# Attention units reordered: slot projection, output projection and gates at other places in the program

## What is computed

```python
q, k, v = heads(x @ Wq), heads(x @ Wk), heads(x @ Wv)        # 16 heads, 64 / 64 / 128 wide
s = clip(heads(x @ Ws), -32, 32)                              # 64 slots
z = cumlogsumexp(s); g = exp(z[t-1] - z[t]); p = exp(s - z)
hk = hk * g_t + k_t p_t;   ok = q_t . hk                      # key state, read by the query
pv = softmax(ok)
hv = hv * g_t + p_t v_t;   ov = pv_t . hv                     # value state
o = ov * rsqrt(mean(ov^2) + eps) * g_norm_weight
o = o * (g * sigmoid(g))                                      # g = x @ Wg
out = x + o @ Wo
```

## Time and profile before

| | |
|---|---|
| median of 3 runs | 2107.34 us (2104.89 to 2109.28) |
| the profiled execution: its time | 2111.22 us |
| the profiled execution: its span | 2109.5 us |
| PE busy | 1982.6 us, 94% of the span |
| DVE / ACT / POOL busy | 65% / 32% / 13% |
| one piece of attention weights: upper half on ACT / lower half on POOL | up to 1.07 / 2.40 us |
| granted PE clock, 1594 to 1597 / 1597 to 1600 / 1600 to 1603 us (last pair) | 0.88 / 0.50 / 0.50 |
| granted PE clock, 1639 to 1642 / 1642 to 1645 us (last pair) | 0.77 / 0.66 |
| attention, as PE sees it | from about 468 to 1681 us of the span |

### The profile page before, as it was taken

One profiled execution on the slowest core, in us unless ns is written; L12 is line 12 of the kernel. 1 busy time (PEld: TensorE's weight loads), 2 busy tenths in 40 slices (PEclk: granted clock), 3 DMA queues, 4 the chain that ended last, 5 costly groups with the idle time before them and its releaser, 6 DMA issues. The chain is left out here.

```text
span 2109.5 us, 29738 instructions
## 1 busy us (share of the span) xinstructions
PE 1982.6 (94%) x11848; PEld 1629.8 (77%) x11848; DVE 1365.2 (65%) x2702; ACT 669.6 (32%) x1207; POOL 278.8 (13%) x216
## 2 busy tenths in 40 slices
PE   2999999969999999999999999999999689999998
PEld 1788888847888888888888888888887468888786
DVE  5765667736667666666766666666767766665684
ACT  2443445514222131221222221221212144443562
POOL 3110111011011020120110110210201200110100
PEclk9999999979999999999999999999999889999999
DMA  6463436660010010010000100100100155443565
GB/s 219 131 199 120 136 119 180 204 195 9 1 38 9 1 38 8 9 31 9 21 25 1 38 9 1 38 8 1 38 1 21 40 169 191 130 110 110 150 187 183
DMA packets 54329, 165.04 MB, mean 78 GB/s; under 512 B 5424, under 2 KB 5424, under 8 KB 54192
## 3 DMA queue, kind: packets, MB, share of 16 engines
q1 hardware_dynamic: 46736, 145.80, 21.1%
q0 software_dynamic: 7456, 17.34, 4.0%
HBM read 137.40 MB, written 25.72 MB: 77 GB/s over the span
## 5 line engine op out<-in xcount | busy, mean ns | idle before, releaser
L1227 PE MATMUL at_pj<-at_w_lo,at_xT_hi 128*128 128x512 f32 x512 | 210.5, 411 | 0.0
L1227 PE MATMUL at_pj<-at_w_hi,at_xT_lo 128*128 128x512 f32 x512 | 202.3, 395 | 0.0
L1227 PE MATMUL at_pj<-at_w_hi,at_xT_hi 128*128 128x512 f32 x512 | 202.3, 395 | 0.0
L1201 PE MATMUL at_pj<-at_xT_hi,at_w_lo 128*128 128x512 f32 x384 | 158.4, 412 | 7.6 <-DVE at_gate L1004 4.9
L550 DVE TENSOR_TENSOR last_ff_w_lo<-last_ff_stage,last_ff_w_hi 128x1024 fp32r<-128x1024 f32 x80 | 97.9, 1224 | 90.4 <-ACT last_ff_w_hi L373 90.2
L1201 PE MATMUL at_pj<-at_xT_hi,at_w_hi 128*128 128x512 f32 x384 | 152.3, 397 | 0.0
L1201 PE MATMUL at_pj<-at_xT_lo,at_w_hi 128*128 128x512 f32 x384 | 151.4, 394 | 0.0
L933 ACT ACTIVATE at_ok<-at_ok 128x512 f32<-128x512 f32 x32 | 20.3, 633 | 412.2 <-DVE at_ok L1122 412.2
L550 DVE TENSOR_TENSOR first_ff_w_lo<-first_ff_stage,first_ff_w_hi 128x1024 fp32r<-128x1024 f32 x80 | 97.9, 1224 | 77.7 <-ACT first_ff_w_hi L373 76.3
L840 POOL TENSOR_TENSOR at_coef<-at_ms,minus_half 128x4 f32<-128x4 f32 x64 | 63.5, 1008 | 559.8 <-DVE at_ms L1164 559.8
L825 POOL TENSOR_TENSOR at_w_lo<-at_stage,at_w_hi 128x1024 fp32r<-128x1024 f32 (+1 forms) x36 | 78.1, 2170 | 380.3 <-ACT at_w_hi L879 380.3
(11 more groups left out here) (315 smaller groups left out, 4783.7 us busy)
## 6 DMA issues: line engine op xcount, KB each, us to landing
first_ff_stage<-wff SPq DMA_DIRECT2D x90, 512.0 KB
last_ff_stage<-wff SPq DMA_DIRECT2D x90, 512.0 KB, 3.9
at_stage<-watt SPq DMA_DIRECT2D x24, 512.0 KB, 3.7
at_stage<-watt SPq DMA_DIRECT2D x16, 384.0 KB, 3.2
xres<-x SPq DMA_DIRECT2D x4, 1024.0 KB, 9.8
mid_rows<-xres SPq DMA_DIRECT2D x4, 1024.0 KB
out<-xres SPq DMA_DIRECT2D x4, 1024.0 KB
first_ff_xg<-sorted_rows SPq DMA_DIRECT2D x3, 1028.0 KB, 5.4
```

Source lines behind the costliest of these rows:

```text
L1201: last = pe.matmul(PJ[(7 * k + part) % 2][:, :], wq(w, kk, part), x[:, kk, tok], start=(kk == 0 and n == 0), stop=(kk == KC - 1 and n == 2))
L1227: last = pe.matmul(PJ[(7 * k + 3 + t) % 2][:, :], x[:, kk, tok], wvg(w, kk), start=(kk == 0 and n == 0), stop=(kk == KC - 1 and n == 2))
```

## The change

Four moves, and their waits:

1. On PE `project_s` of the next unit stands ahead of the read of the key state (L1336), not behind it; DVE takes `s_clip` right behind the sums of the value state, and ACT takes `e_exp` right behind `q_scale`, ahead of the softmax exponential.
2. On PE `project_out` of the unit before stands behind the read of the key state, not between `project_q` and `project_k`; it writes R[0] and R[3] in place of R[2] and R[3]. DVE takes the four adds behind the scaling of the read and ahead of the maximum. The wait for `added` moves from L1326 to the softmax transposes L1350 (which write R[3]).
3. `gate_make` 2 and 3 stand ahead of both lower halves `uT_lo` on DVE, and `vg_read(3)` ahead of both upper halves on ACT.
4. On DVE `z_scan` stands behind the small product of the denominators, ahead of the masks.

```diff
 # ScalarE
                     if more:
                         q_scale(i, k + 1)
+                        e_exp(i, k + 1)
...
+                    if more:
+                        vg_read(i, k + 1, 3)
                     for b in range(2):
-                        if more and b == 1:
-                            vg_read(i, k + 1, 3)
                         act.wait_ge(u_tr, count(i, k, 2, b))
 # VectorE
-                    dve.tensor_tensor(xres[:, k * UC + cc, :], R[2 + cc % 2][:, :], xres[:, k * UC + cc, :], ALU.add).then_inc(added, 1)
+                    dve.tensor_tensor(xres[:, k * UC + cc, :], R[3 * (cc % 2)][:, :], xres[:, k * UC + cc, :], ALU.add).then_inc(added, 1)
...
                     dve.reciprocal(rzT[:, :], zT[:, :]).then_inc(rz_done, 1)
-                    if (i, k) != (0, 0):
-                        add_out(*((i, k - 1) if k else (i - 1, UNITS - 1)), last_pair and k > 0)
                     if more:
                         k_copy(i, k + 1)
...
+                    if more:
+                        s_clip(i, k + 1)
+                    dve.wait_ge(ok_mm, count(i, k, 1, 0))
+                    dve.wait_ge(rz_done, count(i, k, 1, 1))
+                    dve.tensor_tensor(pT[:, :], R[2][:, :], rzT[:, :], ALU.mult).then_inc(ok_scaled, 1)
+                    if (i, k) != (0, 0):
+                        add_out(*((i, k - 1) if k else (i - 1, UNITS - 1)), last_pair and k > 0)
...
+                    if more:
+                        z_scan(i, k + 1)
                     if last_pair and k > 0:
                         unit_statistics(k - 1)
...
+                    if more:
+                        gate_make(i, k + 1, 2)
+                        gate_make(i, k + 1, 3)
                     for b in range(2):
-                        if more and b == 1:
-                            gate_make(i, k + 1, 2)
                         dve.wait_ge(u_hi, count(i, k, 2, b + 1))
 # TensorE
                         project_q(i, k + 1)
-                    if (i, k) != (0, 0):
-                        project_out(*((i, k - 1) if k else (i - 1, UNITS - 1)), True)
-                    if more:
                         project_k(i, k + 1)
...
-                    pe.wait_ge(added, count(i, k, UC, 0))
                     pe.wait_ge(a_masked, count(i, k, 2, 2))
...
+                    if more:
+                        project_s(i, k + 1)
                     pe.wait_ge(hk_done, i * HK_AT[UNITS] + HK_AT[k + 1] + 1)
...
-                    if more:
-                        project_s(i, k + 1)
+                    if (i, k) != (0, 0):
+                        project_out(*((i, k - 1) if k else (i - 1, UNITS - 1)))
                     pe.wait_ge(ok_scaled, count(i, k, 1, 1))
...
+                    pe.wait_ge(added, count(i, k, UC, 0))
                     pe.wait_ge(pv_done, count(i, k, 1, 1))
```

More of the change, by code:

```diff
@@ L934, in pair @@
                     if more:
-                        e_exp(i, k + 1)
                         vg_read(i, k + 1, 0)
-                    if more:
                         vg_read(i, k + 1, 1)
@@ L1122, in pair @@
                     dve.tensor_tensor(by_head(ok[:, :, :]), by_head(turned_ok), spread(highest), ALU.subtract).then_inc(ok_shifted, 1)
-                    if more:
-                        s_clip(i, k + 1)
                     dve.wait_ge(pv_done, count(i, k, 1, 1))
@@ L1143, in pair @@
                         gate_make(i, k + 1, 1)
-                        z_scan(i, k + 1)
                     if last_pair and k > 0:
@@ L1181, in pair @@
                     if more:
-                        gate_make(i, k + 1, 3)
                         kn_copy(i, k + 1)
@@ L1278, in scores, with project_out @@
                             last.then_inc(a_mm, 1)
-            def project_out(i, k, next_masked):
+            def project_out(i, k):
                 if k == 0:
                     pe.wait_ge(piece_lo, i * NP + 1 + 5)
-                if next_masked:
-                    pe.wait_ge(a_masked, count(i, k + 1, 2, 2))
                 if i == PAIRS - 1 and k > 0:
@@ L1293, in project_out @@
                         for n, (x, w) in enumerate(((uT_lo, w_hi), (uT_hi, w_lo), (uT_hi, w_hi))):
-                            last = pe.matmul(R[2 + cc % 2][:, :], x[:, cc // 2, h, (cc % 2) * P:(cc % 2 + 1) * P], wo(w, h),
+                            last = pe.matmul(R[3 * (cc % 2)][:, :], x[:, cc // 2, h, (cc % 2) * P:(cc % 2 + 1) * P], wo(w, h),
                                              start=(h == 0 and n == 0), stop=(h == 1 and n == 2))
@@ L1393, in pair @@
                     else:
-                        project_out(i, k, False)
+                        project_out(i, k)
             for i in range(PAIRS):
```

3 lines of the change are left out of this document (removed).

## The result

The changed kernel takes 2078.65 us, median of four runs (2078.07 to 2081.09), beside 2108.31 us for the kernel before on the same chip (four runs, 2104.89 to 2111.34). The ratio is 0.9862, with an interval of 0.9844 to 0.9880: 29.7 us faster. 2079 had been predicted. The span of the profiled execution went from 2109.5 to 2079.3 us.

A forecast was written before the change was run, and what follows sets the result against it. PE bounds the kernel, so only its waits can go: 12.3 + 6.6 + 7.5 - 0.9 + 2.8 = 28.3 us off 2111.2 gives 2082.9, and 2079 as median. Forecast 2072 to 2084 (0.68), ends 2070 and 2093.

The forecast's parts named there:

- What bounds the kernel: PE, busy 144.53 of 146.40 us in four middle units, sets the pace; only its waits, 1.13 us a unit, can go.
- The query projection: PE's wait for gate 2 ahead of this projection, 13.0 us, goes; 12.3 us won.
- `u`: PE's wait for the second half of `u`, 0.24 us each time, goes with the scan moved: 6.6 us won.
- The key sums and the joins: PE's 0.43 us wait for the key sums goes, less 0.19 for two joins, over 31 units: 7.5 us won.
- The second join: PE leaving a float32 matmul group: the second 512 column matmul comes 0.32 behind, not 0.23; costs 0.09 us.
- The first join: PE going into a plain float32 matmul group: 0.33 us from start to start, not 0.23; costs 0.10.
- The maximum: DVE, behind the four output adds: can start at T + 1.03, T being the last output matmul's start; exponential follows.
- The cover: Slack between the softmax exponential's end and PE's weight load for the softmax transposes: 0.08 us, costed at nothing.
- rival (a): DVE's adds and maximum reach PE late: 2082 to 2098; chance 0.14 below its turning point, 0.04 beyond.
- The other queues: ACT and POOL: weight pieces delayed by `e_exp` stay hidden, piece 3 with 1.8 us to spare; no cost.
- The ends: First unit loses 0.9 us; last pair wins 2.6 and 2.4, loses 1.2 and 1: together 1.9 won.
- the clock's 0 to 4.8 us: Last pair: shorter waits may keep PE at 2.4 GHz, worth 0 to 4.8 us; 2.4 taken.

The follow-up runs named there:

- gates_only: Kernel before with only gates 2 and 3 and the fourth tanh moved ahead of the halves: 2092.66 us, ratio 0.9931.
- scan_only: Kernel before with only the scan moved ahead of the masks: 2104.68 us, ratio 0.9984.
- late_200: Changed kernel with an unused 128-column DVE addition ahead of the maximum in each unit: 2079.22 us, ratio 0.9863.
- slot_only: Kernel before with only the slot projection ahead of the key-state read, its clip and exponential moved along: 2162.80 us, ratio 1.0255.
- out_only: Kernel before with only the output projection, its adds and banks moved as in the changed kernel: 2114.72 us, ratio 1.0027.
- no_scan: Changed kernel with the scan put back behind the masks and gate 1: 2089.10 us, ratio 0.9905.
- slot_piece_first: slot_only with `e_exp` put back behind the weight pieces on ACT: 2130.72 us, ratio 1.0118 to the kernel before.
- after_again: The changed kernel run once more, nothing altered: 2078.61 us, ratio 0.9863.
- late_statistics: Changed kernel with the last tile's statistics, in the last pair, moved from ahead of the maximum to behind the subtraction: 2077.44 us, ratio 0.9849.
- best: late_statistics plus, in the very last unit, the output projection ahead of the key sums in banks 2 and 3: 2078.45 us, ratio 0.9859.
- no_slot: Changed kernel with the slot projection back behind the key-state read and output projection, `s_clip` behind the scaling: 2086.64 us, ratio 0.9895.
- late_600: Changed kernel with an unused 512-column DVE addition ahead of the maximum in each unit: 2093.54 us, ratio 0.9928.

## Why the prediction came out

**What bounds the kernel.** Right: the change took no work away and won 29.7 us. In the middle units all of it was PE's waiting; some 2 us more in the last pair are time that PE no longer spends at half clock. That the number was met to 0.4 us is in part luck: the win was 1.4 us larger than forecast, and the median of the kernel before, beside which it was measured, was 1.0 us higher than the one that the forecast started from.

**The query projection.** Forecast 12.3 us, 0.44 a unit; the steps show 0.48, and so do those of gates_only (its whole unit is 0.51 shorter). The list of waits put 0.46 there. It counts the idle time of the weight load and leaves out that a first matmul after a wait is itself drawn out: in the kernel before its second follows by 0.35 (827.49 to 827.84), in the changed kernel by 0.32.

**`u`.** 0.22 a unit against 0.24. The size was right; that it hangs on the gates' move was not seen, and scan_only showed it.

**The key sums and the joins.** 0.28 against 0.24, so right in size, and that by luck, since two errors nearly cancel. The forecast had a wait of 0.43 less 0.19 for the joins. In the steps, the value sums and the read together became shorter by 0.37, and the projections longer by 0.08. The second join was sized right: with the slot projection behind the value sums and the output projection behind the read there are two places instead of one where the second matmul comes 0.34 (792.60 to 792.94) and 0.31 (796.07 to 796.38) behind the first and not 0.23, and this costs 0.08 for the 0.09 forecast. The first join, 0.10 into the read, isn't there: PE took 0.23 into it and not the 0.33 that the earlier trace rows have into the key-state sums. And the wait was worth 0.37, not the 0.43 that the weight loads idled. The Trainium skill (TensorE: Matmul & The Clock Gate, "Step-by-step: what each phase is for") has PE pull weight loads ahead of matmuls in flight where the row groups don't conflict or where the load goes to the background weight buffer, and that would have made the joins free. The prediction told only the first of these two conditions; no run here shows which of them applies. For the step into the read the trace agrees, with 0.23; for the second matmul behind a group of another tile it doesn't, with 0.34 and 0.31.

**The maximum.** Forecast to start at T + 1.03, with T the last output matmul, and the exponential over by T + 3.11. T is 801.49, and the timelines of DVE and ACT have

```profile
801.93 0.69 DVE L1066 TENSOR_TENSOR xres<-at_r,xres 128x512 f32<-128x512 f32 x1 [0.72 <-PE at_r L1291]
802.54 0.68 DVE L1120 TENSOR_REDUCE at_highest<-at_r 128x8 f32<-128x512 f32 x1
```

```profile
803.98 0.63 ACT L934 ACTIVATE at_ok<-at_ok 128x512 f32<-128x512 f32 x1 [0.99 <-DVE at_ok L1122]
```

which is T + 1.05 and T + 3.12. The cover, 0.08 in the forecast, is 0.2: the term taken wrongly is the "some 0.2 us" that the weight load needs ahead of its matmul. It came 0.06 ahead of it in late_200 and 0.03 in late_600. This was the main reason for the chance of rival (a), which deserved less.

**The other queues.** ACT's piece 3 was reckoned hidden with 1.8 us to spare by the output projection, and no wait for `at_w_lo` shows; at the pair change near 620 us POOL is done at 622.06 and PE wants it at 623.84, 1.8 us later. slot_only shows what that cover is worth: without it, 29 us.

**The ends.** The first unit's step from the read to the transposes is 1.07 us, forecast 1.1. In the last pair (waits of PEld, 1560 to 1660 us) `at_u` fell from the 10.6 of the earlier trace rows:

```profile
PEld at_r L1385 <- DVE at_u L1167: 8.4, 6, 4.2
...
PEld at_r L1331 <- DVE at_hk L1095: 2.6, 1, 2.6
```

In steps, the transposes of `u` wait 1.36 and 1.37 us in units 1 and 2, where it was 2.69 and 2.56: 2.5 won, 2.6 forecast. The statistics cost 0.5 in each and not 0.6. Of the clock's 0 to 4.8 us I took half. Both stretches at half clock went, and these units now run at full clock (third number from the end):

```profile
1564.00:1609.00 45.00, 41.69 (x280) 34.44 (x279) 36.08 (x103) 11.95 (x26) 9.20 (x11) 1.00 0.06 24
```

But only the first stretch was worth anything. Behind the first wait for `u`, the steps of the transposes of `u`, e and the keys and of the query projection take 2.3 us more in the kernel before than in scan_only, which has the same order there and full clock. The second stretch stood at the head of the last unit, and there DVE sets the pace. There too scan_only has the order of the kernel before and full clock. These are the first transposes of `u` and the third tile of the output projection, which waits for an add on DVE, in the kernel before and then in scan_only:

```profile
1638.73 0.66 PE L1389 MATMUL at_r<-ident,at_u 128*128 128x128 f32 x4 [2.30 <-DVE at_u L1168]
...
1646.96 0.48 PE L1294 MATMUL at_r<-at_w_hi,at_uT_lo 128*128 128x512 f32 x1 [1.30 <-DVE xres L1067]
```

```profile
1632.80 0.66 PE L1390 MATMUL at_r<-ident,at_u 128*128 128x128 f32 x4 [1.12 <-DVE at_u L1169]
...
1641.03 0.47 PE L1295 MATMUL at_r<-at_w_hi,at_uT_lo 128*128 128x512 f32 x1 [2.63 <-DVE xres L1067]
```

It is 8.23 us in both: what the clock gave back there, PE waited longer for DVE. So the 2.4 us taken for the clock came out by luck: 2.3 from the first stretch and nothing from the second.

The last unit lost 1.5 and not 1, from the start of the turned keys' transposes to the last output matmul (40.3 us before, 41.8 after). PE waits ahead of the sums, ahead of the read (for the reciprocal, 3.34 us on DVE, as foreseen), and for the exponential:

```profile
1611.61 0.57 PE L1313 MATMUL at_r<-at_en,at_kn 128*64 128x64 f32 x12 [1.85 <-DVE at_kn L1008]
...
1616.08 1.18 PE L1331 MATMUL at_r<-at_qT,at_hk 128*128 128x128 f32 x8 [2.36 <-DVE at_hk L1095]
...
1627.96 1.09 PE L1346 MATMUL at_r<-ident,at_ok 128*128 128x128 f32 x4 [3.14 <-ACT at_ok L934]
```

```profile
1617.00:1620.00 3.00, 3.00 (x10) 2.37 (x9) 0.84 (x3) 0.00 (x0) 0.00 (x0) 0.51 0.00 0
```

The table of clocks was not part of the forecast for this unit, and the row above is what it missed: behind two waits close together the output projection runs at half clock for 3.4 us and takes 7.2 us instead of 5.7, so part of what it covers it pays for in its own length. The stretches at half clock that begin behind waits of this unit grew from two of 6.8 us to one of 3.4 and two of 6.8. The first unit lost 0.5 us, units 1 and 2 of the last pair won 5.1 and its last lost 1.5: 3.1 us won. With 27.7 from the middle this makes 30.8, against 30.2 between the two spans; the run-up ahead of the attention was 0.6 us longer in the trace of the changed kernel.

## What to carry to other kernels

Where one engine is busy for 98.7% of the time and its waits are short and come back in every unit, look for work that doesn't depend on what is waited for and put it ahead of the wait; then look at what that work had covered at its old place, and move something else there. Reckon such moves in pairs: the slot projection alone cost 53 us, the output projection alone 5, and together with the gates and the scan they won 30. A half clock that goes is worth nothing where another engine sets the pace behind it. Test the tight place by a delay of known size in front of it, which gives the cover in one run, and prefer the times from step to step to the idle time of the weight loads, which counts idling that costs nothing and misses matmuls that are drawn out.

## What the hardware showed beside this

- A weight load of transposes that came late, with 0.23 us of idle time ahead of it, cost PE nothing (late_200): it started 0.06 us ahead of its matmul, and the matmul was on time.
- DVE starts an instruction that depends on nothing in flight about 0.6 us behind one that takes 0.69 (801.93 to 802.54, 839.86 to 840.46), and 0.20 behind one of 128 columns that takes 0.28.
- After waits of PE of 2.55 to 2.69 us ahead of `u` in the last pair, the clock was granted at half in 11 of 12 places (the traces of before, gates_only, out_only, no_scan, slot_only and slot_piece_first have two each). After waits of 1.36 to 1.38 us it was in none of 14 (after, after_again, late_statistics, best, scan_only, no_slot and late_200), and in one of the two of late_600, where another wait of 1.34 us stands 15 us ahead of each. The one exception of the first kind, in no_scan, follows the same wait of 2.68, so the length of the wait alone doesn't settle it; what does stays open. All these waits are from the start of the matmul ahead to the start of the first transpose.
- Of the 17 us that the gates alone won, 14.3 lie in the middle units and 2.5 in the last three: 1.0 in units 1 and 2 of the last pair, 1.5 in the last. Why the last one gains was not taken apart.
